# Two context attentions: weighted sums and sums of exponentials as split bf16 products, the splits made in place by GpSimd

## What is computed

```python
q = shape(query @ Wq.T + bq)            # (4, 16, 512, 8), query is the normed x
k = shape(key @ Wk.T + bk)              # (4, 16, 154, 8), key and value are the context
v = shape(value @ Wv.T + bv)
q = q / math.sqrt(DH)
scores = jnp.einsum('bhqd,bhkd->bhqk', q, k).astype(jnp.float32)
scores = jnp.where(mask[:, None, :, :], jnp.float32(-1e+18), scores)
attn = jax.nn.softmax(scores, axis=-1).astype(q.dtype)
context = jnp.einsum('bhqk,bhkd->bhqd', attn, v)
```

## Time and profile before

| | us |
|---|---|
| median of 3 runs | 1762.07 |
| lowest, highest | 1761.32, 1762.89 |
| the profiled execution, whole | 1764.95 |
| its span | 1763.1 |

### The profile page before, as it was taken

How to read it: one execution, slowest core, us unless ns; L and a number is a source line. 1 busy time by engine, 2 the same in 40 slices (tenths; PEclk the granted TensorE clock), 3 DMA queues, 4 the chain that set the end, 5 groups by cost and what they waited for, 6 DMA issues and landing times.

```text
span 1763.1 us, 36462 instructions
## 1 busy us (share of the span) xinstructions
PE 1462.7 (83%) x13597; PEld 981.1 (56%) x13597; DVE 1157.8 (66%) x3020; ACT 767.7 (44%) x1520; POOL 815.6 (46%) x1236
## 2 busy tenths in 40 slices
PE   4999999999999977576788799869975885858997
PEld 2777777777777765454665255524443332524555
DVE  5889688877777755535755566554565457587864
ACT  2777667767766634322143355443212443301111
POOL 3789789977766953561246631000001301134430
PEclk9999999999999997865889799989986687879998
DMA  7333321211211211310000000000000000000000
GB/s 264 87 95 92 95 72 48 55 44 45 58 44 44 60 51 57 113 76 1 1 1 8 5 5 1 1 0 1 1 1 0 1 1 1 1 1 1 7 7 12
DMA packets 35476, 64.26 MB, mean 36 GB/s; under 512 B 7535, under 2 KB 25042, under 8 KB 34147
## 3 DMA queue, kind: packets, MB, share of 16 engines
q1 hardware_dynamic: 33831, 59.82, 11.5%
q0 software_dynamic: 1472, 2.12, 0.4%
HBM read 30.63 MB, written 12.66 MB: 25 GB/s over the span
## 4 chain that ended last, share of the span: by engine, by line
PE 62%; DVE 21%; ACT 6%; issue 4%; POOL 4%; DMA 2%; SPq 0%; ACTq 0%; DVEq 0%; POOLq 0%
PE banks L504 16%; PE banks L744 6%; PE banks L772 5%; PE banks L733 5%; PE banks L2146 4%; DVE xn L450 2%; PE banks L2132 2%; PE banks L2058 2%; ACT work L931 2%; PE banks L479 2%; PE banks L2839 2%; PE banks L2099 1%; DVE norm_room L414 1%; PE banks L1422 1%; POOL work L1039 1%
## 5 line engine op out<-in xcount | busy, mean ns | idle before, releaser
L1039 POOL TENSOR_TENSOR work<-work 128x512 bf16<-128x512 f32 (+1 forms) x512 | 358.8, 723 | 77.0 <-ACT work L931 76.1
L816 DVE TENSOR_REDUCE work<-banks 128x1 f32<-128x666 f32 x256 | 216.3, 845 | 65.8 <-PE banks L733 64.0
L444 POOL TENSOR_TENSOR norm_room<-norm_room,minus_half 128x4 f32<-128x4 f32 x48 | 50.2, 1045 | 410.3 <-DVE norm_room L419 409.8
L938 ACT ACTIVATE work<-banks,work 128x666 f32<-128x666 f32 x256 | 208.1, 813 | 33.2 <-DVE work L816 25.5
L931 ACT ACTIVATE work<-banks 128x512 f32<-128x512 f32 x256 | 152.8, 597 | 144.2 <-PE banks L744 143.7
L733 PE MATMUL banks<-work 128*128 128x512 bf16 (+1 forms) x1024 | 188.6, 307 | 3.7 <-DMA work<-work 3.4
L744 PE MATMUL banks<-const,work 128*128 128x128 f32 x1024 | 159.2, 278 | 14.8 <-ACT work L931 11.8
L504 PE MATMUL banks<-work,weights_b 128*128 128x512 bf16 (+1 forms) x840 | 160.2, 350 | 11.7 <-DVE work L2497 4.5
L733 PEld LDWEIGHTS banks<-work 128*128 128x128 bf16 x1024 | 96.1, 98 | 82.8 <-DMA work<-work 4.2
L772 PE MATMUL banks<-work 128*128 128x65 bf16 (+1 forms) x3840 | 136.0, 192 | 3.3 <-POOL work L1039 1.8
L2223 DVE TENSOR_REDUCE work<-banks 128x2 f32<-128x308 f32 x192 | 86.5, 472 | 78.0 <-PE banks L2104 39.9
(11 more groups left out here) (443 smaller groups left out, 3280.1 us busy)
## 6 DMA issues: line engine op xcount, KB each, us to landing
work<-work SPq DMA_DIRECT2D x128, 166.5 KB, 2.9
sorted<-in_pads SPq DMA_DIRECT2D x10, 838.5 KB
weights_b<-in_weights SPq DMA_DIRECT2D x1, 4120.0 KB, 24.3
work<-scratch SPq DMA_DIRECT2D x64, 64.0 KB, 2.0
weights_b<-in_weights SPq DMA_DIRECT2D x1, 2824.0 KB, 9.4
weights_a<-in_weights SPq DMA_DIRECT2D x1, 2056.0 KB, 9.5
weights_a<-in_weights SPq DMA_DIRECT2D x1, 2050.0 KB, 9.5
work<-work SPq DMA_DIRECT2D x32, 64.0 KB, 1.9
```

The lines of the kernel that those rows point to most:

```text
L816: ve.tensor_reduce(self.neg_max[i % 4], self.slot[i % 2][:, 0:KEYS0], AX_X, ALU.max, negate=True).then_inc(self.mark("max"))
L938: ac.activation(self.probs[i % 3], self.slot[i % 2][:, 0:KEYS0], ACT.Exp, bias=self.neg_max[i % 4]).then_inc(self.mark("exp"))
L1039: po.tensor_tensor(parts[:, :, :, 0], exact, parts[:, :, :, 1], ALU.subtract).then_inc(self.mark(event, i - 3))
```

## The change

The weighs use bf16 products instead of fp32 ones. For the weighted sums there are three passes (upper by upper, lower of the values by upper of the exponentials, upper by lower); for the sums of exponentials two (ones by upper and by lower). The four `terms` tiles of a chunk become one strip of 4 x 256 columns. A new item `strip` on GpSimd subtracts, over the whole strip in one instruction and in place, the upper half from the word and writes the result to the lower half; GpSimd does the same for the values of each batch (item `values`, two instructions). GpSimd now walks the same list of items as the others: heads (with the mask) at u - 0.2, the query's lower half at u + 0.12, the transposed mask at u + 1.15 for odd u, the powers at the `measure` items, the values at their item, and a strip after the four terms of each chunk. The strip's position is also counted in the even spread of terms and weighs. A weigh waits for `strip_low` and, in chunk 0, for `values_low`, no longer for the exponentials and values directly.

```diff
@@ -1981,7 +1981,8 @@
         a.keys = [self.place(heads, CTX, dt=BF16) for _ in range(3)]
         a.keys_rest = [self.place(heads, CTX_REST, dt=BF16) for _ in range(3)]
         a.values = [self.place(a.chunks, GROUPS, WIDE) for _ in range(2)]
-        a.terms = [self.place(HALF) for _ in range(TERMS)]
+        a.strips = [self.place(GROUPS, HALF) for _ in range(TERMS // GROUPS)]
+        a.terms = [strip[:, g, :] for strip in a.strips for g in range(GROUPS)]
         a.exact = [self.place(SEQ) for _ in range(2)]
         a.halves = [self.place(2, SEQ, dt=BF16) for _ in range(2)]
         a.q4 = [self.place(GROUPS, SEQ, dt=BF16) for _ in range(2)]
@@ -2017,12 +2018,12 @@
             if h == 0:
                 out.append((u + 0.72, "values", b, 0, 0))
             elif b + 1 < BATCH:
-                out.append((u + 0.12, "query", b + 1, 0, 0))
+                out += [(u - 0.2, "heads", b + 1, 0, 0), (u + 0.12, "query", b + 1, 0, 0), (u + 1.15, "mask_t", b + 1, 0, 0)]
                 out += [(u + 0.6 + 0.1 * g, "rows", b + 1, g, 7) for g in range(GROUPS)]
             out.append((u + 1.28, "lift", u, 0, 0))
             terms = []
             for c in range(a.chunks):
-                terms += [("term", u, c, g) for g in range(GROUPS)]
+                terms += [("term", u, c, g) for g in range(GROUPS)] + [("strip", u, c, 0)]
                 if c:
                     terms.append(("weigh", u, c - 1, 0))
             terms.append(("weigh", u, a.chunks - 1, 0))
@@ -2137,14 +2138,16 @@
             elif what == "weigh":
                 if c == 0:
                     self.bank(pe, 5, "divided", s, u, 1)
-                    pe.wait_ge(*self.at("values", s, b))
-                n, rows_n, _, _ = self.term(a, u, c, GROUPS - 1)
-                pe.wait_ge(*self.at("exp4", s, n))
-                for of_sums in (0, 1):
-                    for g in range(GROUPS):
-                        left = a.block[0:rows_n, c, :] if of_sums else a.values[b % 2][0:rows_n, c, g, :]
-                        m = pe.matmul(self.bank_of(5)[WIDE * g:WIDE * (g + 1), of_sums * HALF:(of_sums + 1) * HALF], left,
-                                      self.term(a, u, c, g)[3], start=c == 0 and not of_sums, stop=c == a.chunks - 1, skip_group_check=True)
+                    pe.wait_ge(*self.at("values_low", s, b))
+                rows_n = self.term(a, u, c, 0)[1]
+                pe.wait_ge(*self.at("strip_low", s, u, c))
+                for of_sums, passes in ((0, ((1, 1), (0, 1), (1, 0))), (1, ((1, 1), (1, 0)))):
+                    for n, (of, at) in enumerate(passes):
+                        for g in range(GROUPS):
+                            left = a.block[0:rows_n, c, :] if of_sums else a.values[b % 2][0:rows_n, c, g, :]
+                            m = pe.matmul(self.bank_of(5)[WIDE * g:WIDE * (g + 1), of_sums * HALF:(of_sums + 1) * HALF], self.halves(left)[:, :, of],
+                                          self.halves(self.term(a, u, c, g)[3])[:, :, at], start=c == 0 and not of_sums and n == 0,
+                                          stop=c == a.chunks - 1 and n == len(passes) - 1, skip_group_check=True)
                 m.then_inc(self.mark("weighed", s, u, c))
             elif what == "finish":
                 bank = self.bank(pe, 7, *brought(u))
@@ -2293,19 +2296,29 @@
                 i = po.memset(mask[:, 1, :], 0.0)
             po.wait_ge(*self.own("po", i))
             self.mask_t_po(po, a, 0)
-            for b in (2, BATCH - 1):
-                self.follow_power(po, 3, b)
-        for b in range(1, BATCH):
-            if s == 4:
-                self.mask_po(po, b)
-            self.heads_of(po, a, b)
-            self.query_low(po, a, b)
-            if s == 4:
-                if b >= 2:
-                    self.follow_power(po, 4, b - 2)
-                self.mask_t_po(po, a, b)
-        if s == 4:
-            self.follow_power(po, 4, BATCH - 2)
+        for what, u, c, g in self.context_items(a):
+            if what == "heads":
+                if s == 4:
+                    self.mask_po(po, u)
+                self.heads_of(po, a, u)
+            elif what == "query":
+                self.query_low(po, a, u)
+            elif what == "mask_t" and s == 4:
+                self.mask_t_po(po, a, u)
+            elif what == "values":
+                v = a.values[u % 2]
+                po.wait_ge(*self.at("values", s, u))
+                for part in (v[:, 0:a.per_group, :, :], v[0:a.rest, a.per_group:a.chunks, :, :]):
+                    whole = part.rearrange("p c g n -> p (c g n)")
+                    i = po.tensor_tensor(self.halves(whole)[:, :, 0], whole, self.halves(whole)[:, :, 1], ALU.subtract)
+                i.then_inc(self.mark("values_low", s, u))
+            elif what == "strip":
+                n, rows_n, _, _ = self.term(a, u, c, GROUPS - 1)
+                po.wait_ge(*self.at("exp4", s, n))
+                whole = a.strips[(u * a.chunks + c) % len(a.strips)][0:rows_n, :, :].rearrange("p g n -> p (g n)")
+                po.tensor_tensor(self.halves(whole)[:, :, 0], whole, self.halves(whole)[:, :, 1], ALU.subtract).then_inc(self.mark("strip_low", s, u, c))
+            elif what == "measure":
+                self.follow_power(po, u, c)
```

More of the change, by code:

```diff
@@ L197 @@
         "clear": "filled", "unless": "filled", "cleared": "filled", "bias_parts": "filled", "up_low": "low_b", "down_low": "low_b", "hidden_low": "low_b",
-        "qkv_kept": "q_high", "product": "low_b", "x_based": "low_b", "shares": "ve", "weighted": "ve", "multiplied": "ve", "centred_x": "ve", "tokens": "filled", "four_times": "filled", "wo_low": "filled", "mixed_low": "low_b", "summed": "router_steps", "ranked": "routed",
+        "qkv_kept": "q_high", "product": "low_b", "x_based": "low_b", "shares": "ve", "weighted": "ve", "multiplied": "ve", "centred_x": "ve", "tokens": "filled", "four_times": "filled", "wo_low": "filled", "mixed_low": "low_b", "strip_low": "low_b", "values_low": "low_b", "summed": "router_steps", "ranked": "routed",
         "places": "placed", "tile_stats": "ve", "gathered": "low_b", "padded": "router_steps", "relative": "router_steps", "delta": "router_steps",
```

## The result

The changed kernel takes **1834.39 us** in the median of four runs (1832.74 to 1837.2), against 1762.48 of the kernel before in the same comparison: a ratio of 1.040, with an interval of 1.038 to 1.043. The forecast was 1805, from 1774 to 1826. The sign and TensorE's waits came as told; the size did not: the measured time lies 8 us beyond the end of the range.

A forecast was written before the change was run, and what follows sets the result against it. TensorE was taken to bound both attention loops, with everything walking one ordered list. Product savings, split waits, the start's gain and side effects summed to +32.7 us (stage 4) and +10.7 (stage 6), +43 together: 1805 us, range 1774 to 1826.

The forecast's parts named there:

- The products: Weighs in stages 4 and 6: five bf16 rounds save 0.32 us each, -13.0 and -9.4 us.
- The rival in which the rounds do not shorten: Weighs: loads of 32 columns bind and a round stays 0.216 us; 1829 us in all, chance 0.08.
- The split: GpSimd's subtraction over 1024 columns ahead of each weigh: 1.90 us, bounds 1.04 and 2.3.
- The waits: TensorE's weighs held by GpSimd's splits and the work queued ahead of them: 41.7 us in stage 4, 18.1 in stage 6.
- last chunks: Last weigh of each half-batch waits for its split: +13 us in stage 4, 10.2 of +11.4 in stage 6.
- heads: Next batch's mask and heads between splits of chunks 2 and 3 stop TensorE: +17 us in stage 4, +5.7 in stage 6.
- The start: Stage 4's start: heads and query go ahead of a norm's power, removing most of a 5.94 us wait: -4 us.
- Side effects: VectorE slowed beside busy GpSimd, +3 us; lower clock after two 8.4 us waits, +5 in stage 4, +2 in stage 6.
- the clock goes down for good: Rival: stage 4 runs a third of its time at 1.2 GHz, +15 us, 1820 us in all; chance 0.12.
- The unchanged rest: Code after the two stages depends on them only through their end, so it adds nothing.
- Only the ends of the halves cost: Rival: TensorE's stop at the heads is made up by VectorE and ScalarE running ahead; about 1771 us, chance 0.10.
- splits are hidden: Rival: splits land before TensorE asks, so only the savings count; 1736 us, chance 0.05.

The follow-up runs named there:

- order in pieces: Kernel before with GpSimd's heads, masks and query cut into pieces and moved, fp32 products, no subtractions: 1751.53 us, 0.994; with upper-half bf16 products, no subtractions: 1734.47 us.
- part 7: The kernel before run once more for its trace alone, to compare the unchanged stretch after stage 6: 1756.26 us.
- part 4: GpSimd's work in pieces, upper-half bf16 products only; with subtractions nobody reads 1734.81 us, 0.986, without them 1734.47 us, 0.984, against the kernel before.

## Why the prediction was wrong, step by step

Stages of the traces, TensorE's busy time and its waits for the split:

| | stage 4 | PE busy | clock | stage 6 | PE busy | clock | waits |
|---|---|---|---|---|---|---|---|
| before (two traces) | 161.0, 160.7 | 144 | 0.97 | 109.5, 105.2 | 94, 90 | 0.82, 0.86 | 0 |
| order in pieces, fp32 | 153.8 | 142 | 0.98 | 105.2 | 90 | 0.86 | 0 |
| the same, bf16, no split | 141.1 | 130 | 0.98 | 93.5 | 77 | 0.91 | 0 |
| order of the change, no split | 142.7 | 131 | 0.97 | 102.2 | 88 | 0.77 | 0 |
| the same, split, nobody waits | 151.1 | 133 | 0.96 | 113.0 | 97 | 0.68 | 0 |
| the change | 200.5 | 148 | 0.86 | 135.6 | 104 | 0.64 | 41.6 + 17.6 |

- **The products**: forecast -13.0 and -9.4; 153.8 to 141.1 and 105.2 to 93.5 are -12.7 and -11.7 (the second with the clock going from 0.86 to 0.91). Right. The rival in which the rounds do not shorten is out.
- **The split** at 1.90 us, right. The larger estimate from the Trainium skill (GPSIMD Engine Reference, Performance versus the Vector engine), 2.2 us, does not hold for this form: 1.90 us was measured for 1024 columns.
- **The waits**: forecast 41.7 and 18.1 (last chunks, heads, transposed mask, query, values together), measured 41.6 and 17.6. Right, in stage 4 also in their places. That the sums fit so closely is partly luck: the fourth of stage 4's terms in size was an allowance, and in stage 6 heads 2.2 us too cheap and last chunks 2.5 us too dear made up for each other.
- **The start**: forecast -4. Without splits the first half-batch takes 34.3 us in place of 42.6, of which 2.8 are what bf16 products change in the order in pieces (35.4 and 32.6). Right. In the changed kernel itself the waits for the split hide it, 40.2 us.
- **Side effects, the step that failed.** Its terms were +3 for VectorE and +5 and +2 for the clock, "bounds 0 and 20". In the order in pieces the products took TensorE's busy time down by 12 us in each stage (142 to 130, 90 to 77). The changed kernel's should be 132 us (144 less 12) and 77 us. It is 148 and 104: 16 us and 27 us more, where the sum had 5 and 2 for the clock. That it is the clock is seen in busy time times clock, which hardly moves (127 in both kernels in stage 4, 66 and 70 in stage 6). Since the 77 us ran at 0.91 and the kernel before at 0.82 to 0.86, the loss in stage 6 against the kernel before is 18 to 22 us (estimated with the 70). The rest of the stages adds up with it: -12.7 + 41.6 + 16 and about -5 at the start make +40, measured +39.5; -11.7 + 17.6 + 26.5 make +32 against the second trace of before, measured +30.4.
- **Where the clock went**, by TensorE's busy time down the last four rows. Stage 4: 130, 131, 133, 148, so the loss came with the waiting for the splits, 15 us where the forecast had 5. Stage 6: 77 in pieces, 88 in the order of the change, 97 with the load, 104 with the waiting. Only 7 of the 27 us came with the waits that the forecast tied its term to; the other 20 were there before any product waited for a split. What links them to the order and the load stays open.
- Why I sized it so: the 5 and 2 were priced as an aftermath of the two longest waits alone. The rival "the clock goes down for good" was nearer in kind, a lower clock over the whole stage, but with +15 for stage 4 only and nothing for stage 6, which lost more.
- **The unchanged rest**, forecast 0: +7.6 between these two traces; the 284 and 291 us come in kernels of every kind, and the cause is open (part 7).
- "Only the ends of the halves cost" is out (the 8.46 us wait); "splits are hidden" is out. That GpSimd's load would hurt VectorE was right as a mechanism (scaling 973 ns against 456 in the two kernels of part 4), while its +3 us is neither borne out nor refuted: with nobody waiting, the whole load costs between nothing and some 11 us in the order in pieces.

## What to carry to other kernels

When a helper engine is put between two steps of the bounding engine, price the queue before the load: the same subtractions cost little in one order (0.3 us in the medians, 11 at most by the estimate above) and some 17 in another before anyone waits for them, and 72.7 more once a product does. Ask of each product which of its passes need the helper's result, and whether the helper can be reordered at all before giving it work: here reordering, with no new arithmetic, gave the fastest version that computes the reference. And where the clock is already below full, do not price its loss by the longest waits alone: in stage 6 TensorE's products grew by 27 us, 20 of them in runs in which no product waited for a split. A run that keeps the new order and leaves the waiting out shows this before the waits are counted.

## What the runs showed of the hardware that I had not expected

- A VectorE copy with source and destination in SBUF, 16 columns wide, did not end before GpSimd was through a row of seven instructions: 7.10 us in place of 0.17. With the copy gone, the subtraction behind it took 2375 ns in the mean. Reductions from PSUM in the same stage kept 470 ns. With GpSimd's instructions in pieces and the same subtractions, the copy took 428 ns in the mean of stage 6.
- With the same TensorE instructions and no wait for a split, stage 6 had a granted clock of 0.91, 0.88, 0.77 and 0.68 in four traces of kernels that differ in GpSimd's order and load alone. The runs do not show what links them.
- The 290 us behind stage 6, the same code in every kernel, take 284 or 289 to 292 us, at clocks of 0.88 or 0.85.
